# First attention's logits by a split product of float32r parts in place of a full float32 product

## The reference, cut to what matters

```python
Wh = einsum('bnf,hfo->bhno', x, W)            # 4 heads, 512 -> 512
f1 = einsum('bhno,ho->bhn', Wh, a[:, :O])     # the logits
f2 = einsum('bhno,ho->bhn', Wh, a[:, O:])
e = leaky(f1[:, :, :, None] + f2[:, :, None, :]); e = where(adj > 0, e, -1e9)
h = elu(einsum('bhnm,bhmo->bhno', softmax(e), Wh))
out = elu(gat(concat_heads(h), adj, W_out, a_out))
y = relu(out @ w1 + b1) @ w2 + b2 + out
result = layernorm(x + layernorm(y) * gamma + beta)
```

## Time and profile before

| | us |
|---|---|
| median of 3 executions | 2170.45 (2170.04 to 2170.59) |
| the profiled execution | 2170.8 |
| its span in the trace | 2169.0 |
| TensorE busy | 2125.0 (98%) |
| VectorE busy | 1590.4 (73%) |
| GpSimd busy | 958.3 (44%) |
| ScalarE busy | 949.7 (44%) |

### The profile page before, as it was taken

One profiled execution on the slowest core, in us unless ns is written; L12 is line 12 of the kernel. 1 busy time (PEld: TensorE's weight loads), 2 busy tenths in 40 slices (PEclk: granted clock), 3 DMA queues, 4 the chain that ended last, 5 costly groups with the idle time before them and its releaser, 6 DMA issues.

```text
span 2169.0 us, 42902 instructions
## 1 busy us (share of the span) xinstructions
PE 2125.0 (98%) x13860; PEld 1923.6 (89%) x13860; DVE 1590.4 (73%) x3202; ACT 949.7 (44%) x2186; POOL 958.3 (44%) x1015
## 2 busy tenths in 40 slices
PE   5999999999999999999999999999999999999997
PEld 2899999999999999999999999999999988999997
DVE  3867776677777767677677777777777669999998
ACT  2544444444444444444444444444444443434443
POOL 3633333333333333333333333333333337777776
PEclk7999999999999999999999999999999999999999
DMA  8011111111111111111111111111111133333342
GB/s 287 30 40 40 39 39 39 39 39 39 39 39 39 39 39 39 39 39 39 39 40 42 40 39 39 39 39 39 39 39 40 44 108 128 134 126 135 121 140 87
DMA packets 73861, 134.04 MB, mean 62 GB/s; under 512 B 8672, under 2 KB 8800, under 8 KB 73824
## 3 DMA queue, kind: packets, MB, share of 16 engines
q1 hardware_dynamic: 73824, 133.57, 18.4%
HBM read 99.98 MB, written 33.55 MB: 62 GB/s over the span
## 4 chain that ended last, share of the span: by engine, by line
PE 93%; POOL 1%; issue 1%; DVE 1%; ACT 0%; DMA 0%; POOLq 0%; DVEq 0%; SPq 0%; ACTq 0%
PE h_ps L415 11%; PE h_ps L417 11%; PE h_ps L416 11%; PE t_ps L431 11%; PE t_ps L430 11%; PE t_ps L429 11%; PE h_ps L509 3%; PE h_ps L511 2%; PE h_ps L510 2%; PE t_ps L525 2%; PE t_ps L523 2%; PE x_ps L364 2%; PE t_ps L524 2%; PE x_ps L399 1%; PE x_ps L400 1%; PE h_ps L400 1%
## 5 line engine op out<-in xcount | busy, mean ns | idle before, releaser
L1075 POOL TENSOR_TENSOR h_lo<-h_full,h_hi 128x256 fp32r<-128x256 f32 x512 | 391.8, 765 | 1045.5 <-ACT h_hi L672 1036.1
L415 PE MATMUL h_ps<-g_hi,wh_hi 128*128 128x256 f32 x2048 | 587.4, 287 | 1.8 <-DVE h_full L893 1.3
L417 PE MATMUL h_ps<-g_hi,wh_lo 128*128 128x256 f32 x2048 | 578.9, 283 | 0.0
L416 PE MATMUL h_ps<-g_lo,wh_hi 128*128 128x256 f32 x2048 | 578.1, 282 | 0.0
L891 DVE TENSOR_SCALAR h_full<-h_full 128x256 f32<-128x256 f32 x512 | 281.6, 550 | 359.0 <-ACT h_full L643 357.8
L431 PE MATMUL t_ps<-wo_hi,h_lo 128*128 128x512 f32 x1024 | 403.6, 394 | 0.0
L430 PE MATMUL t_ps<-wo_lo,h_hi 128*128 128x512 f32 x1024 | 403.2, 394 | 0.0
L429 PE MATMUL t_ps<-wo_hi,h_hi 128*128 128x512 f32 x1024 | 401.9, 393 | 0.0
L415 PEld LDWEIGHTS h_ps<-g_hi,wh_hi 128*128 128x128 f32 x2048 | 386.7, 189 | 16.9 <-DVE h_full L893 2.4
L416 PEld LDWEIGHTS h_ps<-g_lo,wh_hi 128*128 128x128 f32 x2048 | 385.7, 188 | 13.3
L417 PEld LDWEIGHTS h_ps<-g_hi,wh_lo 128*128 128x128 f32 x2048 | 386.1, 189 | 0.0
(11 more groups left out here) (122 smaller groups left out, 3837.2 us busy)
## 6 DMA issues: line engine op xcount, KB each, us to landing
x_dup<-in_x SPq DMA_DIRECT2D x248, 128.0 KB, 2.6
attn<-in_x_t SPq DMA_DIRECT2D x64, 256.0 KB, 2.8
mid<-o_buf SPq DMA_DIRECT2D x64, 256.0 KB, 2.0
o_in<-mid SPq DMA_DIRECT2D x32, 512.0 KB, 3.6
x_again<-in_x SPq DMA_DIRECT2D x32, 512.0 KB, 4.3
out<-res SPq DMA_DIRECT2D x64, 256.0 KB, 2.0
wt_raw<-in_w_heads_t SPq DMA_DIRECT2D x4, 1024.0 KB, 9.5
wh_raw<-in_w_heads SPq DMA_DIRECT2D x4, 1024.0 KB, 17.0
```

The costliest lines, as they stand in the source:

```text
L415: mm(to, w_hi, g_hi[:, h, ft, :], start=ft == 0, stop=False)
L416: mm(to, w_hi, g_lo[:, h, ft, :], start=False, stop=False)
L417: last = mm(to, w_lo, g_hi[:, h, ft, :], start=False, stop=ft == FT - 1)
L1075: tt(h_lo[:, v % RING, :], h_full[:, v % 2, :], h_hi[:, v % RING, :].bitcast(F32), ALU.subtract).then_inc(h_lo_done, 1)
```

## The change

The logits become a product in parts with the operands exchanged. `u` is split into `u_split`, 16 columns for each of the four feature tiles (8 high, 8 low), laid ahead of `same_batch` in one tile `u_then_batch`; a 128 column slice of it that begins at feature tile ft is the weights. The transposed x is split by ScalarE (`x_t_round`) and VectorE (`x_t_rest`, the low part overwrites the raw data) and is the moving operand: 256 columns for each of two parts and four feature tiles, in two halves (`half_logits`). The result has the logits in its rows, so ScalarE copies it out (`f_rows_out`), TensorE transposes it with two 128x128 transposes (`logits_of`), and VectorE adds the high and low rows in `logits_out`.

Where the steps of chunk c+1 stand in iteration c:

| step | engine | before | after |
|---|---|---|---|
| `x_t_round` | ACT | - | v 0, 2 (after the extra of the second attention, ahead of `h_hi`) |
| `x_t_rest` | DVE | - | v 0, 2 (after `logits2_of`) |
| `half_logits` | PE | - | after head 1; at v 3 after `add_out` and `spread2` |
| `f_rows_out` | ACT | - | v 4, after `x_round` |
| `logits_of` | PE | v 1 | v 4 (now only the transposes) |
| `logits_out` | DVE | v 2 | v 5, four instructions instead of three |
| `diagonal` | POOL | v 3 | v 5, after `x_rest` |
| `spread` | PE | v 5 | v 7 |
| scores, softmax | DVE | v 5 to 10 | v 7 to 11 |
| `exps` | ACT | v 8 | v 10, after `x_round` |
| `transpose_attn` | PE | v 12 | v 13 |
| `attn_t_round`, `attn_t_rest` | ACT, DVE | v 13, 14 | v 14, 15 |

`h_full` gets four buffers that lie in the memory of `h_lo`, so that GpSimd's low part overwrites it; ScalarE's wait for `h_lo` becomes a wait for `add_out(v-4)`, and the wait ahead of `h_hi` goes. At the start of the kernel ScalarE splits the first transposed x and copies the first logits out ahead of its other work.

```diff
+            def half_logits(c, k):
+                pe.wait_ge(x_t_lo_done, c * 2 + k + 1)
+                if k == 0:
+                    after(pe, g_lo_done, c * GQ - 1)
+                for f in range(2):
+                    ft = 2 * k + f
+                    parts = u_then_batch[:, ft * 4 * NH:ft * 4 * NH + P]
+                    hi = x_t_first[:, ft, :, :] if first_of(c) else x_t_hi[:, f, :, :]
+                    mm(x_ps[0][:, 0:T], parts, hi, start=ft == 0, stop=False)
+                    last = mm(x_ps[0][:, 0:T], parts, x_t_lo[:, :, ft, :], start=False,
+                              stop=ft == FT - 1)
+                last.then_inc(logits_half, 1)
             def logits_of(c):
-                pe.wait_ge(x_t_in, (c + 1) * CP * 16)
-                after(pe, g_lo_done, c * GQ - 1)
-                for p in range(CP):
-                    for ft in range(FT):
-                        last = mm(x_ps[0][:, p * 2 * NH:(p + 1) * 2 * NH],
-                                  attn_flat[:, p * F + ft * P:p * F + (ft + 1) * P], u[:, ft, :],
-                                  start=ft == 0, stop=ft == FT - 1)
+                pe.wait_ge(f_rows_done, c + 1)
+                for p in range(CP):
+                    part = slice(p * P, (p + 1) * P)
+                    last = transpose(x_ps[0][:, T:2 * T][:, part], f_rows[:, part], ident[:, :])
                 last.then_inc(logits_ps, 1)
...
                         if v == 1:
+                            half_logits(c + 1, 0)
+                        if v == 3:
+                            half_logits(c + 1, 1)
+                        if v == 4:
                             logits_of(c + 1)
-                        if v == 5:
+                        if v == 7:
                             spread(c + 1)
-                        if v == 12:
+                        if v == 13:
                             transpose_attn(c + 1)
...
+            def x_t_round(c, k):
+                act.wait_ge(x_t_in, (c + 1) * CP * 16)
+                if k == 0:
+                    act.wait_ge(logits_ps, c)
+                else:
+                    act.wait_ge(logits_half, c * 2 + 1)
+                act.activation(x_t_hi[:, :, :, :], x_t_raw[:, 2 * k:2 * k + 2, :, :], copy).then_inc(x_t_hi_done, 1)
+            def f_rows_out(c):
+                act.wait_ge(logits_half, c * 2 + 2)
+                act.activation(f_rows, x_ps[0][:, 0:T], copy).then_inc(f_rows_done, 1)
...
-                    after(act, h_lo_done, c * TILES + v - 1)
-                    act.activation(h_full[:, v % 2, :], h_ps[v % 2][:, 0:T], exp).then_inc(h_exp, 1)
+                    after(act, t_done, c * TILES + v - LAG)
+                    act.activation(h_full[:, v % RING, :], h_ps[v % 2][:, 0:T], exp).then_inc(h_exp, 1)
...
                         if v in (1, 4, 7, 10):
                             x_round(c + 1, v // 3)
+                        if v in (0, 2):
+                            x_t_round(c + 1, v // 2)
+                        if v == 4:
+                            f_rows_out(c + 1)
...
+            act.wait_ge(x_t_in, CP * 16)
+            for k in range(2):
+                act.activation(x_t_first[:, 2 * k:2 * k + 2, :, :], x_t_raw[:, 2 * k:2 * k + 2, :, :], copy)\
+                    .then_inc(x_t_hi_done, 1)
+            f_rows_out(0)
             act.wait_ge(x_first_in, 32)
...
+            def x_t_rest(c, k):
+                dve.wait_ge(x_t_hi_done, c * 2 + k + 1)
+                hi = x_t_first[:, 2 * k:2 * k + 2, :, :] if first_of(c) else x_t_hi[:, :, :, :]
+                tt(x_t_lo[:, :, 2 * k:2 * k + 2, :].rearrange("p a f n -> p f a n"),
+                   x_t_raw[:, 2 * k:2 * k + 2, :, :], hi.bitcast(F32), ALU.subtract).then_inc(x_t_lo_done, 1)
```

More of the change, by code:

```diff
@@ L108, in build @@
             pass
+        with nc.sbuf_tensor("x_t_lo", [P, CP, FT, P], F32R) as x_t_lo:
+            pass
         attn = sb("attn", [P, 2, CP, NH, N])
@@ L116, in build @@
         g_lo = sb("g_lo", [P, NH, FT, T], F32R)
-        h_full = sb("h_full", [P, 2, T])
+        with nc.sbuf_tensor("f_buf", [P, CP, P], F32) as f_buf:
+            pass
+        x_t_hi = sb("x_t_hi", [P, FT // 2, CP, P], F32R)
         h_hi = sb("h_hi", [P, RING, T], F32R)
+        with nc.sbuf_tensor("h_full", [P, RING, T], F32) as h_full:
+            pass
         h_lo = sb("h_lo", [P, RING, T], F32R)
@@ L215, in build @@
         block = ctx.enter_context(nc.Block())
+        u_split = u_then_batch[:, 0:FT * 4 * NH].rearrange("p (f s k) -> p f s k", f=FT, s=2)
+        same_batch = u_then_batch[:, FT * 4 * NH:FT * 4 * NH + P]
         f2_hi, f2_lo = (s[:, :].rearrange("p (a h) -> p a h", a=CP) for s in (row_max, row_sum))
+        x_t_raw = attn[:, :, :, :, :].rearrange("p d a h n -> p (d a h n)")\
+            .rearrange("p (a f n) -> p f a n", a=CP, f=FT)
+        f_rows = f_buf[:, :, :].rearrange("p a n -> p (a n)")
         attn_flat = attn[:, :, :, :, :].rearrange("p d a h n -> p (d a h n)")
@@ L559, in _ @@
             pe.wait_ge(u_done, 1)
+            half_logits(0, 0)
+            half_logits(0, 1)
             logits_of(0)
@@ L670, in iteration @@
                     act.wait_ge(h_elu, c * TILES + v + 1)
-                    after(act, t_done, c * TILES + v - LAG)
-                    act.activation(h_hi[:, v % RING, :], h_full[:, v % 2, :], copy).then_inc(h_hi_done, 1)
+                    act.activation(h_hi[:, v % RING, :], h_full[:, v % RING, :], copy).then_inc(h_hi_done, 1)
             def weights_round(ft):
@@ L889, in iteration @@
                     dve.wait_ge(h_exp, c * TILES + v + 1)
-                    full = h_full[:, v % 2, :]
+                    full = h_full[:, v % RING, :]
                     ts(full, full, 1.0, -1.0, ALU.min, ALU.add).then_inc(h_min, 1)
@@ L1014, in _ @@
             nc.vector.memset(attn2_bd[:, :, :], 0.0)
+            for k in range(2):
+                x_t_rest(0, k)
             dve.wait_ge(folded, 1)
@@ L1074, in iteration @@
                     pool.wait_ge(h_hi_done, c * TILES + v + 1)
-                    tt(h_lo[:, v % RING, :], h_full[:, v % 2, :], h_hi[:, v % RING, :].bitcast(F32),
-                       ALU.subtract).then_inc(h_lo_done, 1)
+                    tt(h_lo[:, v % RING, :], h_full[:, v % RING, :], h_hi[:, v % RING, :].bitcast(F32), ALU.subtract)\
+                        .then_inc(h_lo_done, 1)
                     if first and v < 2 * FT:
```

56 lines of the change are left out of this document (33 added, 23 removed).

## The result

The changed kernel takes 2352.08 us, the median of four executions (2339.41 to 2358.91), against 2170.28 before: a ratio of 1.0831, 95% interval 1.0785 to 1.0877. The forecast was 2321, range 2285 to 2368: right in sign and mechanism, 31 us short in size, nearly all of that from the clock. The time lies above the prediction's main case (2292 to 2345) and inside only the wider range, which had room for falls of the clock and for later waits. The profiled execution took 2358.91, with a span of 2357.1.

The account below looks back on a forecast made before the run. TensorE, busy 98% of the span, was taken to bound the kernel. Middle chunks 143.1, iteration 0 6 and the start 0.8 make 150 us, which on 2170.8 gives 2321 us, range 2285 to 2368.

Parts of the forecast that it names:

- The products: TensorE's logits work: 1.78 us of old work replaced by 1.22, saving 0.56 us for each of 31 chunks, 17 us.
- Wait 1: After head 1, TensorE waits for VectorE's low part of the first half of x: 2.01 us late.
- Wait 2: At tile 4, TensorE waits for f_rows_out, which ScalarE issues behind x_round(1), itself standing for the DMA: 2.5 us.
- rule on the port: Two-SBUF-input VectorE and GpSimd instructions exclude each other: wait as long as the overlap, up to 0.36, sum 5 us higher.
- Wait 3: At tile 15, the gather on TensorE waits for VectorE's attn_t_rest(1): 0.41 us, with restart 0.52, bounds 0 and 0.8.
- later waits taken as 0: Diagonal at tile 5 before spread: 0, up to 0.9; exps at tile 10: 0, up to 1 without cover.
- The chunk: A middle chunk costs 4.25 us up to head 5 plus 0.52 at the gather: +4.77 us, 30 of them 143.1.
- Iteration 0: First iteration: the existing diag wait stays at 2.0 and both large waits are new: +6 us, bounds 4 and 8.
- (a): TensorE's clock falls in the new waits: 2411 if in each middle chunk, 2351 in one of three; chance 0.16.
- (b): The waits are covered and the kernel gets 17 us faster: 2153; chance 0.04.
- (c): Only one of the two large waits binds: +3.8 us a chunk, 2292; chance 0.09.
- (d): VectorE and GpSimd meet more often, spread late by 0.9: +5.7 us a chunk, 2349; chance 0.08.

Follow-up runs that it names:

- e10: The changed kernel's whole chain reordered in several steps, lastly GpSimd's diagonal of the second attention put ahead of h_lo(3): 2161.93 us, ratio 0.9966 to the kernel before.
- e2: Changed kernel with ScalarE copying the logits rows out ahead of x_round at tile 4, nothing else: 2283.23 us, ratio 1.0526.
- e7: Changed kernel with both large waits filled by unread products and the attention transposes a tile earlier, exponentials at tile 9: 2293.82 us, ratio 1.0571.
- e3: Changed kernel with the first low part made earlier and used after head 2, and the rows copied out ahead of x_round: 2241.05 us, ratio 1.0331.
- e4: Changed kernel with both large waits of TensorE filled by 15 and 18 products nobody reads: 2320.14 us, ratio 1.0697.
- e6: Kernel before the change with only the four h_full buffers sharing h_lo's memory and the two changed waits: 2170.20 us, ratio 1.0001.
- e9: Changed kernel with both large waits only half filled, by 8 and 9 products nobody reads: 2320.66 us, ratio 1.0697.
- e1: Changed kernel with the first low part ahead of VectorE's tile 0 reductions and used after head 2, not head 1: 2324.20 us, ratio 1.0704.

## Why the prediction was right, and where it was off

The prediction counted a wait from the start that a matmul would have had in a full queue; the views show idle time, which is about 0.16 less. The waits below are therefore given by the spacing of starts, as means of 28 middle chunks.

- **The products.** 0.56 us saved a chunk. The kernel nearly without waits, e10, has 0.45, its period still holding 0.17 of stretched spacings at head 2, which waits for the ELU of tile 0. Right.
- **Wait 1.** 2.01 forecast, 2.09 measured (1.93 idle), and 0.10 behind it, where 0.11 was taken (from its own rows that comes out as 0.09). The 0.08 is the hand-over, 0.13 and not 0.05. Right, from one row: VectorE is free at 1024.17.
- **Wait 2.** 2.5 forecast, 2.44 measured (2.27 idle). Right, and e2 shows that it is the place behind `x_round` that makes it. The estimate for VectorE and GpSimd meeting was right too: `h_lo(2)` on GpSimd, before and after, lasts the 0.2 longer that was taken:

```profile
1028.01 0.73 POOL L1075 TENSOR_TENSOR h_lo<-h_full,h_hi 128x256 fp32r<-128x256 f32 x1 [1.19 <-ACT h_hi L672]
1028.51 0.93 POOL L1141 TENSOR_TENSOR h_lo<-h_full,h_hi 128x256 fp32r<-128x256 f32 x1 [3.15 <-ACT h_hi L718]
```

  The prediction's rule on the port, a wait as long as the overlap, came out too long: in the middle iterations `x_t_rest` and this `h_lo` overlap by 0.34, and `h_lo` is 0.21 longer. Its bound of 0.36 is also 0.02 more than its rows give (1.10 less 0.765).
- **Wait 3.** 0.41 forecast, 0.72 measured (0.56 idle). Two parts of 0.17 each were missed: VectorE itself stands for ScalarE's copy of the transposed attention, and from VectorE's end to TensorE's start it takes 0.23, not 0.06 (1072.59 to 1072.82). e7 prices the wait at 26 us in all.

```profile
1071.19 1.40 DVE L869 TENSOR_TENSOR attn_t_lo<-x_ps,attn_t_hi 64x512 fp32r<-64x512 f32 x2 [0.17 <-ACT attn_t_hi L650]
```
- **The later waits taken as 0** were 0 in the changed kernel: no wait for `diag` in its middle. e3 shows how thin that was: the same chain binds as soon as wait 2 goes.
- **The chunk.** 4.77 forecast, 4.83 in the shortest period, 4.87 in e4's median. The sum of the forecast holds a slip of 0.08: head 5 was put 7.35 behind head 2 as before, but 0.08 of that is the slower first matmul behind the old products, which go; 4.69 is what its terms give.
- **Luck in the sum.** e4, the same order without falls of the clock, took 2320, the forecast was 2321. That closeness is luck: the chunk costs 0.1 more, 3 us in all, and the edges cost as much less. For the start 0.8 was to be added. In the eleven traces with the new start the first gather is at 47.16 to 49.32, in the median 48.41, where it was at 48.45: no addition is seen. Iteration 0 cost 3.7 (gather 1 at 107.89 instead of 104.73), not 6, under its lower bound. TensorE waited 0.69 for `diag` there, where 2.0 was to stay.
- **The step that failed: the clock.** "Against it: the 2.21 us gap at 70.4 left it at 1.00", with 0.16 for falls at all and their cost as 3.0 each. One gap that did nothing was read as a bound. Of some 60 gaps of 1.9 to 2.5 us, 26 were followed by a fall, each costing 1.5: 39 us in the profiled execution, and 20 us of spread between executions. TensorE's busy time, which was to be 17 less, is 41 more. That one gap could not bound it, e6 shows: there the same gap of the kernel before, 0.01 longer, was followed by a fall. And in iteration 0 of the changed kernel a gap of 3.22 left the clock at 1.00. Their rows, with the stretches around them:

```profile
71.87 0.89 PE L374 MATMUL x_ps<-diag,same_batch 128*128 128x512 f32 x2 [2.22 <-POOL diag L1056]
72.00:76.00 4.00, 4.00 (x17) 3.71 (x18) 2.98 (x5) 1.06 (x3) 4.00 (x4) 0.57 0.03 8
```
```profile
72.29 0.44 PE L391 MATMUL x_ps<-ident,f_buf 128*128 128x128 f32 x2 [3.22 <-ACT f_buf L639]
68.00:76.00 8.00, 4.78 (x31) 4.01 (x30) 4.29 (x8) 3.16 (x8) 4.45 (x6) 1.00 0.11 34
```

  The Trainium skill, "TensorE: Matmul & The Clock Gate", section "Why this matters for your kernels", wants no gap over about 3 us; here 1.9 us was enough (e2, 20 falls), 1.4 was not (e9), and 3.22 did nothing once. The measurement decides.
- **The rivals.** (a) came true in part: its case of a fall in one chunk of three gives 2351, within 1 us of the measured median, but by luck: per chunk falls came 2.6 times as often (26 in 30) and cost half. (b), that the waits are covered, holds only after the order is changed in some ten places (e10). (c) and (d) did not come: both large waits bind, and `diag` is in time.

## What to carry to other kernels

On a full engine a step that grows from one stage to four must be placed by when each input is ready on the other queues, and what stands ahead of it there: here 0.56 us of cheaper work was bought with 5.4 us of waits, all readable from one iteration of the trace before. A wait removed alone often comes back at the next place of the same chain (e1, e3), so fix the chain, and judge it by the period of the loop. Count a wait as the idle time that the view shows plus about a quarter us, and once gaps come near 2 us, add falls of the clock; one gap that left the clock alone is no evidence that the next will.

## What was not expected of the hardware

- Filling the waits with useless matmuls made the kernel faster by 32 us (2352 to 2320), through the granted clock: the periods are those of chunks without a fall. Half as many did the same.
- Longer gaps weren't followed by more falls. e1 with gaps of 2.7 us had 12 falls in some 28 chunks, four of them twice as long (6.8 us), e2 with gaps of 1.9 had 20. The gap of 3.22 above had none, nor had gaps of 2.8 in iteration 0 of e2 and e3, while one of 1.83 in e3 had one. What beside its length decides whether a gap is followed by a fall stays open.
- A gap costs more than its idle time: 0.15 ahead of the first matmul behind it, since the last one before the gap still lasts 0.39 where its turn in a full queue is 0.23, and 0.10 behind it (1072.82 to 1073.04 where 0.12 is the rule).

```profile
1072.82 0.38 PE L424 MATMUL h_ps<-attn_t_hi,x_split 128*128 128x256 f32 x1 [0.57 <-DVE attn_t_lo L869]
```
